# Reordering GpSimd's work per pair of attention units, and the entry into attention, in a fused Flamingo block

## The reference

```python
Q = (q @ Wq.T).reshape(b, s, 8, 4, 128)          # q = layernorm(x), 32 heads
K = (k @ Wk.T).reshape(b, s, 8, 128)             # k = v = ctx, 8 groups
V = (v @ Wv.T).reshape(b, s, 8, 128)
scores = einsum('bqhed,bkhd->bheqk', Q, K) * scale, causal mask
probs = softmax(scores)
attn = einsum('bheqk,bkhd->bqhed', probs, V)
x = x + tanh(g_xattn) * (attn.reshape(b, s, 4096) @ Wd.T)
x = x + tanh(g_ffn) * ffn(layernorm(x))          # three linears with w * (su @ sv)
```

## Time and profile before

| | |
|---|---|
| median of 3 runs | 1430.93 us (1430.73 to 1432.84) |
| the profiled execution, its own time | 1430.72 us |
| its span in the trace | 1428.7 us |
| TensorE busy | 1400.6 us, 98% of the span |
| GpSimd busy | 1038.6 us, 73% |
| VectorE busy | 1016.2 us, 71% |
| ScalarE busy | 640.3 us, 45% |

### The profile page before, as it was taken

How to read it: one execution, slowest core, us unless ns; L and a number is a source line. 1 busy time by engine, 2 the same in 40 slices (tenths; PEclk the granted TensorE clock), 3 DMA queues, 4 the chain that set the end, 5 groups by cost and what they waited for, 6 DMA issues and landing times.

```text
span 1428.7 us, 19944 instructions
## 1 busy us (share of the span) xinstructions
PE 1400.6 (98%) x6810; PEld 1125.3 (79%) x6810; DVE 1016.2 (71%) x1549; ACT 640.3 (45%) x1246; POOL 1038.6 (73%) x919
## 2 busy tenths in 40 slices
PE   8999999999999999999999999999999999999998
PEld 8988788888887767777776766767888888888887
DVE  6487777777465677777776776775688878676776
ACT  6465555554444344443443444444344434343433
POOL 5599999998879556656656777775678886666664
PEclk9999999999999999999999999999999999999999
DMA  8477787778887745434443433331112112212112
GB/s 282 150 251 226 233 270 257 253 254 282 307 264 264 254 156 199 140 125 142 135 152 118 155 116 120 127 132 31 45 45 60 52 45 65 105 47 65 45 59 74
DMA packets 116067, 217.96 MB, mean 153 GB/s; under 512 B 9472, under 2 KB 47616, under 8 KB 113920
## 3 DMA queue, kind: packets, MB, share of 16 engines
q1 hardware_dynamic: 115968, 216.70, 46.1%
HBM read 151.13 MB, written 65.54 MB: 152 GB/s over the span
## 4 chain that ended last, share of the span: by engine, by line
PE 82%; POOL 8%; DVE 4%; issue 3%; ACT 1%; DMA 1%; SPq 0%; DVEq 0%; POOLq 0%; ACTq 0%
PE bank L574 65%; PE bank L848 3%; PE bank L849 3%; PE bank L850 3%; PE bank L697 3%; PE bank L722 3%; POOL prob L1663 2%; POOL xn L1677 1%; POOL wd_lo L1649 1%; POOL prob L1657 1%; POOL prob L1669 1%; DVE X L1386 1%; POOL wa_lo L1643 1%; PE bank L621 1%; DMA q_sb<-q_scratch 0%
## 5 line engine op out<-in xcount | busy, mean ns | idle before, releaser
L574 PE MATMUL bank<-xc,wa_hi 128*128 128x512 f32 x896 | 277.4, 391 | 0.0
L574 PE MATMUL bank<-wd_hi,o_hi 128*128 128x512 f32 x512 | 207.9, 406 | 5.0 <-issue 3.5
L574 PE MATMUL bank<-wd_lo,o_hi 128*128 128x512 f32 x512 | 200.8, 392 | 0.0
L574 PE MATMUL bank<-wd_hi,o_lo 128*128 128x512 f32 x512 | 199.5, 390 | 0.0
L574 PEld LDWEIGHTS bank<-xc,wa_hi 128*128 128x128 f32 x896 | 167.7, 188 | 36.4 <-issue 1.1
L574 PE MATMUL bank<-xc,wa_lo 128*128 128x512 f32 x448 | 174.5, 390 | 0.0
L1455 DVE SCALAR_TENSOR_TENSOR X<-bank,tg,X 128x512 f32<-128x512 f32 x221 | 154.5, 742 | 0.0
L574 PE MATMUL bank<-x_hi,wf_hi 128*128 128x512 f32 x392 | 153.0, 390 | 0.0
L574 PE MATMUL bank<-x_hi,wf_lo 128*128 128x512 f32 x392 | 152.6, 389 | 0.0
L574 PE MATMUL bank<-x_lo,wf_hi 128*128 128x512 f32 x364 | 141.7, 389 | 0.0
L1669 POOL TENSOR_TENSOR prob<-prob,row_inv 128x512 f32<-128x512 f32 x64 | 72.5, 1153 | 94.6 <-DVE row_inv L1356 94.6
(11 more groups left out here) (181 smaller groups left out, 3424.7 us busy)
## 6 DMA issues: line engine op xcount, KB each, us to landing
q_scratch<-q_st SPq DMA_DIRECT2D x32, 1024.0 KB, 4.4
q_sb<-q_scratch SPq DMA_DIRECT2D x64, 512.0 KB, 4.9
w_raw<-in_wq SPq DMA_DIRECT2D x32, 512.0 KB, 4.4
wd_raw<-in_wd SPq DMA_DIRECT2D x16, 1024.0 KB, 5.1
f_raw<-ffn_eff_scratch SPq DMA_DIRECT2D x28, 512.0 KB, 3.6
er_raw<-in_sf_r SPq DMA_DIRECT2D x42, 256.0 KB, 3.9
e_raw<-in_wf SPq DMA_DIRECT2D x42, 256.0 KB, 5.4
ffn_eff_scratch<-e_eff SPq DMA_DIRECT2D x42, 256.0 KB, 5.2
```

The source lines that it names most:

```text
L574: last = pe.matmul(to, a, b, start=(start and n == 0), stop=(stop and n == 3 * len(pairs) - 1), skip_group_check=onto)
```

## The change

It moves code on four engines; no instruction is added or dropped.

```diff
@@ TensorE: behind the last quad
+        output(0)
         weighted_values(1)
-        output(0)
@@ ScalarE: behind out_hi(0)
         other_maxima(1)
+        out_hi(1)
         exponentials(2)
         exponentials(3)
         other_sums(1)
-        out_hi(1)
@@ VectorE: quad(q), behind t2
+            if q == NQ - 1:
+                maxima(2)
+                maxima(3)
+                v.wait_ge(a_tanh, 1)
+                out_lo(0)
@@ VectorE: behind the quads, and in the loop over pairs
-        v.wait_ge(a_tanh, 1)
-        out_lo(0)
-        maxima(2)
-        maxima(3)
         row_maxima(1)
+        out_lo(1)
         sums(2)
...
             add_to_x(2 * u - 8)
-            out_lo(u - 3)
+            if p > 2:
+                out_lo(u - 3)
@@ GpSimd: in the loop over pairs
             masked(u)
             masked(u + 1)
+            less_max(u)
+            less_max(u + 1)
             if p in COLUMNS1:
                 x2_sums(COLUMNS1[p])
             if p in WD_STEP:
                 k, heads = WD_STEP[p]
                 for e in heads:
                     output_lo(k, e)
-            less_max(u)
-            less_max(u + 1)
```

## The result

| | before | after |
|---|---|---|
| median | 1431.88 us (1430.73 to 1434.05, 4 runs) | 1452.22 us (1451.02 to 1453.92, 4 runs) |
| span of the profiled execution | 1428.7 us | 1450.4 us |

The change made the kernel slower: the ratio is 1.0141, 95% interval 1.0124 to 1.0159. The forecast was 1449 us in a range of 1441 to 1455.

The account below looks back on a forecast made before the run. TensorE was taken to bound ordinary pairs, so every new wait is paid in full. Terms 7.9 + 6.1 - 4.1 + 2.5 + 5.2 - 1.0 + 1.6 = +18.2 us gave 1449 us, range 1441 to 1455.

Parts of the forecast that it names:

- The mechanism: Odd pairs: `row_max`, paced by TensorE, holds `less_max`; moving it up only puts `wd_lo` behind it, and TensorE waits.
- Ordinary odd pairs: Pairs 3, 5, ... 17: output begins 0.99 us later because `wd_lo` ends late; eight times, +7.9 us.
- Pairs 19 and 25: Odd pairs with column sums: sums and `wd_lo` follow `less_max`, next scores 3.06 us later; twice, +6.1 us.
- Pairs 21 to 23 and 27 to 29: Scores of 23 and 29 come 2.1 us earlier, -4.1 in all; new waits within pairs 23 and 29, +2.5.
- Pair 31: `wd_lo` ahead of pair 30's feed-forward weights delays GpSimd about 2.4 us; pair 31's output starts late, +5.2 us.
- The clock: TensorE's half clock behind long waits: one fall goes, -1.6 us; two new falls, +3.3; together +1.6.
- The entry: Start of attention: four VectorE instructions moved up let the scores of pair 3 begin earlier, -1.0 us.
- The Wd load: `load_wd` in odd pairs is released at 595.9 instead of 590.5; costed at nothing unless landing takes over 7.6 us.
- cover holds: Rival: `wd_lo` is ready in time after all, only gains remain: -14.3 us, 1416 us; chance 0.05.

Follow-up runs that it names:

- odd ordinary pairs alone: Kernel before, with `less_max` ahead of `wd_lo` only in odd pairs 3 to 17: 1440.29 us, ratio 1.0059.
- even pairs alone: Kernel before, with `less_max` ahead of column sums and `wd_lo` only in even pairs 2 to 28: 1425.97 us, ratio 0.9958.
- one head in odd pairs: Changed kernel, with weights of three heads made in even pairs and of one head in odd pairs: 1441.94 us, ratio 1.0064 to the kernel before.
- the loop alone: Kernel before with only the GpSimd edit, `less_max` ahead of column sums and `wd_lo` in all pairs, old entry: 1452.19 us, ratio 1.0141.
- pairs 19 and 25 alone: Kernel before, with `less_max` ahead of column sums and `wd_lo` only in pairs 19 and 25: 1441.99 us, ratio 1.0071.
- the entry alone: Changed kernel with `less_max` back in its old place, the other edits kept: 1432.38 us, ratio 1.0004 to the kernel before.
- pairs 30 and 31: Kernel before, with `less_max` ahead of `wd_lo` only in pairs 30 and 31: 1437.45 us, ratio 1.0034.

## Why the prediction was right, point by point

**The mechanism.** Its steps on who waits for whom held; the terms that were off are below. `row_max` is paced by TensorE, `less_max` did not move in ordinary pairs, `wd_lo` did, and TensorE has no slack there. The run with odd ordinary pairs alone, the one with even pairs alone and the one with one head in odd pairs show it from three sides.

**Ordinary odd pairs.** 0.99 forecast, 1.07 measured per pair. `wd_lo` ended 13.13 us behind the scores (598.76 - 585.63), as worked out; what was missed is about 0.1 us that the products lose around a restart (the first one took 0.47 for 0.39).

**Pairs 19 and 25.** The output was to be 4.25 late and was 4.05 and 3.8. Less the 1.2 us that the scores' own wait had cost, that is 2.9 and 2.6 against 3.06. The rest of 9.5 is clock.

**Pairs 21 to 23 and 27 to 29.** Forecast with the clock: -3.2; measured -4.0. The output of pair 21 was to be 1.36 late and was 1.01: in the old trace `less_max` of pair 21 stood 8.93 us behind the scores, for there `row_max` took 0.51 beside a `wd_lo`, which the change moves away; now it is 8.6. The absorption of pair 21's wait in pair 22 held: 21 and 22 together took 32.2 us, as they did in the kernel with only the sums moved, which has no such wait.

**Pair 31.** The output was to be 5.2 late and was 4.0 (16.39 us behind the scores, 12.36 before). The mis-sized step is "`less_max` goes from 976.30 to 978.7": it came 11.7 us behind the scores, not 12.8. I had read pair 30 from the old trace, where its `less_max` was 8.9 behind the scores, not the 8.6 of an ordinary pair and of the new trace, and `row_max` of pair 31 took 0.76 there and 0.19 now.

**The clock.** This is the term most in error: +1.6 forecast. I took two falls of three, of 1.64 each, less the one that goes. All three fell, and behind them 2.3, 1.7 and 2.8 us were lost: 5.2 net of the one saved. So 1.6 of the 3.6 that were missing is the third fall, and 2.0 is the size. The size does not follow the length of the wait: behind a wait of 5.8 in pair 19 a fall cost 2.3 in the changed kernel, 2.0 with the loop alone and 1.6 with pairs 19 and 25 alone; behind 3.9 in pair 31 it cost 2.8, 2.8 and 1.4. What sets it the runs do not show. One case was not enough to price it.

**The entry.** -1.0 forecast, -0.8 in the traces, too little for the times of the run with the entry alone to show. The Wd load cost nothing: ScalarE waited 6.62 us for it in pair 20 and TensorE none.

That the sum of 18.2 came as close to the measured 20.3 of the medians as it did is in part luck, for two errors have opposite signs: 3.6 too little for the clock, and about 1.7 too much for all the rest (pair 31 alone 1.2). 1.6 us of the profiled difference lie ahead of all edits. Traces of the other kernels here, with the same code up to there, differ by as much: one product near 441 us (L621) starts anywhere from 440.78 to 442.45, and the scores of pair 0 start at 466.60 in the trace with odd ordinary pairs, at 462.03 to 463.70 in all others.

The rival that made the change faster (cover holds) fell as stated: it hung on `row_max` coming 0.99 us sooner. Its worth was real, though. The kernel that keeps `wd_lo` ahead and puts only the sums behind gets 13.2 us of the 14.3 that I had worked out for a change without new waits.

## What to carry to other kernels

Before an item is moved behind a waiting one in a program that is in order, look at what the waiting one waits for. If that is paced by the bound engine, the waiting item gains nothing and the moved one is late by the whole wait. Then ask who needs the moved item, and how soon: here the sums could wait for a pair, and the weights for about 4.4 us only (done at 590.52, wanted 0.21 ahead of 595.08). Of a group of items moved together, move each alone once; the half of this change that was good was worth 11 to 13 us, and the other half hid it.

A wait of the bound engine can cost more than its length: here the clock fell behind every wait of 3.1 us and more in attention, at 1.4 to 2.8 us each.

## What the runs showed of the hardware

Behind each of the eleven waits of TensorE of 3.1 to 5.8 us ahead of these outputs (three in the changed kernel, three with the loop alone, two with pairs 19 and 25, three with three heads and one), and behind the one of 3.9 with pairs 30 and 31, 4 us read from TensorE's restart show a granted clock of 0.50 to 0.65. Behind the twelve waits of about 2.75 us ahead of the scores of 23 and 29 (two in each of six traces) it fell seven times: behind one of two in the kernel before and in four other runs, behind both with pairs 19 and 25 alone. These seven falls cost 1.6 to 1.7 us each, those behind the longer waits about 1.4 to 2.8. Shorter waits, of 0.8 to 1.8 us, were followed by a clock of 1.00 in all 80 cases but one: in the trace with odd ordinary pairs the wait of 1.76 at the entry was followed by 0.66.

The releaser that the list names for a wait on several semaphores can be a bystander: "DVE X" ended last, but the output followed `wd_lo`.

VectorE's `row_max` and `row_sum` (two inputs of 128x32 each, 0.18 to 0.19 us by themselves) last longer when they start beside certain operations of GpSimd. In the 12 traces 136 of them took over 0.25 us, up to 1.22. Each of the 136 had started while GpSimd was in a `wd_lo`, `xb` or `fs` operation, and each ended 0.04 to 0.06 us behind the end of a GpSimd operation that was running at its start. So a small operation of VectorE on the critical chain is to be read from a place where GpSimd is doing what it will do after the change.
